# Moving the second-expert matmuls of FFN block 3 behind the third level's second half in a fused RWKV-7 and expert-FFN kernel

## What is computed

```
xn  = layernorm(x)
s   = timemix(xn)             # RWKV-7: mixes, LoRA gates, a recurrence over time, group norm
      S_t = S*decay + (S a) b^T + v k^T ;  y_t = S_t r
g   = silu(ffn(xn))
      top 2 of 8 experts by softmax of xn @ gate_w
      for each chosen expert e:  relu(xn@wi + bi + (xn@A_e)@B_e) @ wo + bo, times the sum of the two scores
```

## Time and profile before

| quantity | value |
|---|---|
| median of 3 runs | 990.77 us (990.7 to 991.04) |
| the profiled execution | 991.04 us, with a span of 989.2 us from first to last instruction |
| PE busy | 973.3 us, 98% of the span |
| DVE busy | 837.0 us, 85% |
| ACT busy | 637.8 us, 64% |
| POOL busy | 441.1 us, 45% |
| granted TensorE clock, mean | 1.000 of full speed (2.4 GHz) |

### The profile page before, as it was taken

The page is one execution under the profiler, slowest core; times in us unless marked ns, Lnnn a source line. Parts: engine busy times, 40 slices in busy tenths (PEclk is TensorE's granted clock), DMA queues, the critical chain, the costliest instruction groups (busy, mean ns, idle before and its releaser), DMA issues.

```text
span 989.2 us, 46773 instructions
## 1 busy us (share of the span) xinstructions
PE 973.3 (98%) x20578; PEld 766.3 (77%) x20578; DVE 837.0 (85%) x1685; ACT 637.8 (64%) x1483; POOL 441.1 (45%) x536
## 2 busy tenths in 40 slices
PE   8999999999999999999999999999999999999997
PEld 5777778787787877777777787877878777787775
DVE  7988979789798897979979798897988979789776
ACT  4765765756757566676656667577575666756655
POOL 4452724427154361634627245372443716346150
PEclk9999999999999999999999999999999999999999
DMA  8000000000000000000000000000000000000000
GB/s 261 14 3 3 4 3 24 4 23 4 17 10 4 24 4 23 4 4 23 4 24 3 3 24 3 24 4 3 24 4 25 3 24 3 4 24 4 13 4 23
DMA packets 9416, 17.28 MB, mean 17 GB/s; under 512 B 1920, under 2 KB 4224, under 8 KB 8960
## 3 DMA queue, kind: packets, MB, share of 16 engines
q1 hardware_dynamic: 9216, 14.30, 4.5%
HBM read 10.10 MB, written 4.19 MB: 14 GB/s over the span
## 4 chain that ended last, share of the span: by engine, by line
PE 95%; DVE 2%; issue 1%; ACT 1%; SPq 0%; DMA 0%; ACTq 0%; DVEq 0%
PE bank L259 34%; PE bank L258 20%; PE grams L474 10%; PE bank L352 5%; PE bank L489 3%; PE bank L500 3%; PE grams L543 2%; PE grams L448 2%; PE grams L598 2%; PE grams L563 2%; PE bank L574 2%; PE bank L533 2%; PE bank L367 2%; PE bank L584 1%; PE bank L383 1%; PE bank L307 1%
## 5 line engine op out<-in xcount | busy, mean ns | idle before, releaser
L1272 POOL TENSOR_TENSOR bk<-bk,tot 128x256 f32<-128x256 f32 x192 | 155.4, 817 | 138.1 <-PE grams L474 138.1
L1594 DVE COPY_PREDICATED gm<-c_mask_g,grams 128x1024 f32<-128x1024 int32 x96 | 161.3, 1680 | 5.7 <-PE grams L474 3.9
L1026 ACT ACTIVATE gl<-gm 32x128 f32<-32x128 f32 x320 | 99.1, 310 | 78.3 <-DVE gm L1594 72.1
L917 ACT ACTIVATE relu<-bank,prm 128x256 f32<-128x256 f32 x256 | 105.7, 472 | 36.7 <-PE bank L259 34.2
L1253 POOL TENSOR_TENSOR xd<-mtmp,xnc 128x512 f32<-128x512 f32 x95 | 121.1, 1276 | 13.1 <-DVE mtmp L1455 11.3
L474 PEld LDWEIGHTS grams<-ar,bk 64*64 64x64 f32 x6144 | 102.2, 134 | 19.5 <-issue 14.4
L259 PE MATMUL bank<-w_wo,hid 128*128 128x256 f32 x488 | 116.1, 386 | 0.0
L474 PE MATMUL grams<-ar,bk 64*64 64x64 f32 x6144 | 110.2, 220 | 0.0
L1604 DVE TENSOR_TENSOR ar<-ar,tot 128x512 f32<-128x512 f32 x96 | 92.5, 964 | 13.2 <-PE grams L474 13.2
L259 PEld LDWEIGHTS bank<-w_wo,hid 128*128 128x128 f32 x488 | 90.1, 190 | 13.1
L259 PE MATMUL bank<-xnc,w_wi 128*128 128x256 f32 x392 | 94.4, 384 | 0.9 <-ACT relu L917 0.9
(11 more groups left out here) (247 smaller groups left out, 2150.8 us busy)
## 6 DMA issues: line engine op xcount, KB each, us to landing
x_in<-x SPq DMA_DIRECT2D x16, 256.0 KB, 2.9
out<-out_t SPq DMA_DIRECT2D x15, 256.0 KB, 2.0
w_wi<-w_wi_dram SPq DMA_DIRECT2D x1, 1024.0 KB, 7.0
w_wo<-w_wo_dram SPq DMA_DIRECT2D x1, 1024.0 KB, 9.3
w_lora_B<-w_lora_B_dram SPq DMA_DIRECT2D x1, 512.0 KB, 8.2
w_x_B<-w_x_B_dram SPq DMA_DIRECT2D x1, 384.0 KB, 3.2
w_kW<-w_kW_dram SPq DMA_DIRECT2D x1, 256.0 KB, 4.4
w_rW<-w_rW_dram SPq DMA_DIRECT2D x1, 256.0 KB, 4.0
```

The source lines that it names most:

```text
L917: A(dst[:, p % 2, j * 256:(j + 1) * 256], ZB[p % 2][:, j * 256:(j + 1) * 256], ACT.Relu, bias=prm[:, P_BI + 2 * p + j:P_BI + 2 * p + j + 1 ...
L1026: A(gl[l % 2][o:o + 32, :, :, :].rearrange("p q g (c n m) -> p (q g c) n m", c=2, m=m), right(gm[o:o + 32, :, :, :, b, 0, 32 * k:32 * k + ...
L1272: tt(v, v, d, ALU.mult).then_inc(S(f"bk{k}_scaled"), 1)
L1594: run(v.copy_predicated(dst, msk.to_broadcast([128, 32, HALF // m, m]), src), "g_stored")
```

## The change

In the branch of steps 2 to 16, PE's `diff(3)` is taken from its place between `gram(4)` and `kW` and put behind `inv_off(3)`, ahead of `gram(5)`. No other engine's order is changed, and no wait is added or removed.

```diff
                     if rec:
                         gram(4)
-                        diff(3)
                     if front:
                         pe.wait_ge(*till("mx_4_done", 2))
                         kW()
                     if rec:
                         inv_x(3)
                     if front:
                         pe.wait_ge(*till("mx_5_done", 2))
                         wk_B()
                     if rec:
                         inv_off(3)
+                        diff(3)
                         gram(5)
                         inv_x(4)
                     if front:
                         pe.wait_ge(*till("kraw_done", 1))
                         pe.wait_ge(*till("ksq_done", 1))
                         g_A()
```

## The result

The changed kernel takes 1032.76 us (median of 4 runs, 1028.41 to 1033.59). The kernel before took 990.9 beside it. The ratio is 1.0407, with a 95% interval of 1.0391 to 1.0424: 4% slower. The forecast was 1020.8, with a range up to 1027. The direction was right and the size too small by 12 us.

What follows compares the result with a forecast made beforehand. PE, never idle in a full step of 60.08 us, was taken as the bound. 14 x 1.97 + 2.38 = 29.96 us on the median of 990.77 gave 1020.8 us, with a range of 1010 to 1027.

Steps and rivals of the forecast that it cites:

- What bounds the kernel: PE is busy for all 60.08 us of a full step, so any wait opened on it is added whole.
- The entry of `diff(3)`: Between `inv_off(3)` and `gram(5)`, `diff(3)` pays its own entry from small tiles: 1.06 us in all, 0.20 added per step.
- a free entry: At `diff(3)`, weight loads pulled ahead could make the entry cost nothing, the sum about 3 us smaller over 15 steps.
- The wait before `inv_off(3)`: PE reaches `inv_off(3)` before DVE's `keep_x(3)` is done and waits about 0.14 us, bounded by 0 and 0.25.
- The queue behind `relu(2, 3)`: On ACT, `pack_gram(4)` and `kraw_` wait behind `relu(2, 3)`, so PE waits 1.04 us before `inv_x(4)` and 0.59 before `g_A`.
- The two waits: PE waits 1.04 us for `gl` before `inv_x(4)` and 0.59 us for `ksq` before `g_A`, 15 times each.
- The total at full clock: 14 steps longer by 1.97 us and step 2 by 2.38, added to the median of 990.77: 1020.8 us.
- "The granted clock stays 1.00": Sign expected in the profile after: PE's granted clock stays at 1.00, with a full step of about 62.05 us.
- The rival in which the clock falls: PE's clock drops to 1.2 GHz around `inv_x(4)` and `g_A`: 22 us over 15 steps, 1042 or more; chance 0.03.
- The range: For the whole kernel's time, 1010 to 1027 us, about 0.87 together; the likeliest case's own range was 1013 to 1026.

Runs made afterwards that it cites:

- the kernel without the queue waits: The changed kernel with ACT's `relu(2, 3)` moved behind `sig_`: 991.32 us, ratio to before 1.0008.
- the four kernels with a filled pause: The changed kernel with useless 256-column matmuls in both of PE's pauses (1018.7 us), the first alone (1020.16), the second alone (1020.42), or half the first (1019.47).

## Why the prediction was right and where it was wrong

- **What bounds the kernel**: right. PE has no idle time in a full step, and every wait that was opened stayed in the total.
- **The entry of `diff(3)`**: right, 1.07 as against 1.06, and `kW` alone 1.92 against 1.93. Against it I had set a free entry, after the Trainium skill's rule on pulled-ahead weight loads ("TensorE: Matmul & The Clock Gate", Part 2: What happens when you issue a matmul). The 0.20 is there, so that reading of the rule doesn't hold for this entry. The rule asks for free rows of the array or the background buffer, and no run here shows whether either was given.
- **The wait before `inv_off(3)`**: its cause right, its size too large. `inv_off(3)` starts 3.35 us after `kW` does (442.95 - 439.60) where 3.48 was worked out. What is left of the 0.14 is 0.02 ahead of it and 0.07 within it, as its piece of the chain lasts 0.45 instead of 0.38. Together with the entry a step grows by 0.28 in the kernel without the queue waits, against 0.34.
- **The queue behind `relu(2, 3)`**: right, and shown by moving one line on ACT. 2.01 us were forecast from the end of `diff(3)`'s matmuls to `gl`, 2.04 measured (444.47 to 446.51). The two waits are 1.10 and 0.58 to 0.61, against 1.04 and 0.59. A step at full clock is 62.2, against 62.05. In step 2 `norm` starts at 68.39, where 68.40 was worked out.
- **The total at full clock**: right, about 1019 to 1020 (both pauses filled, or one), against 1020.8. The extra 0.15 x 15 = 2 us and 3 us fewer of the pauses without a cause nearly cancel.
- **"The granted clock stays 1.00"**: wrong, and this is the miss. The rival in which the clock falls got a chance of 0.03. It is what happened, in 8 of 15 steps, and it costs 12 to 14 us: 1032.76 less 1018.7 to 1020.4 in the four kernels with a filled pause. So the sum lacked a term for the clock. The evidence I held against it was a trace at 1.00 throughout and one row after the end of PE's work, which showed that the clock doesn't fall at once. It said nothing of a stretch in which PE does small pieces between pauses. The kernel before has no such stretch in its full steps, so its trace could not have excluded it, and the chance of the rival was not mine to put at 0.03. Its price was off too, in both directions: I let only `inv_x(4)` and `g_A` run slow, but in every step. In truth `inv_x(4)` is still at full clock, and in the fall shown above all from `g_A` to `norm` is slow, 1.54 us a time, but only in some steps. The Trainium skill's section on frequent short pauses ("TensorE: Matmul & The Clock Gate", A second HAM failure mode: psum-queue depth-cycling) describes this, and here the trace agrees: mean clock 0.985 with pauses of 1.1 and 0.6 us.
- **The range** ended at 1027, since the rival with the clock was left outside. It should have reached to 1042, the price that the text itself gave.

Why some steps keep their clock and others with the same pauses don't is not settled: the order of instructions is the same in them. Nor is the cause of the pauses that carry no releaser, which come to about 4.7 us over 14 steps of the kernel before and to between 0.4 and 1.5 in several of the others.

## What to carry to other kernels

When an instruction is moved later on one engine, look at its reader's own list: what stands behind the reader waits too, needed or not. Count the slack of everything behind it, not of the reader; here the DVE addition that reads `relu(2, 3)` comes more than 10 us later, and `gl`, behind it in the list, had 2.57 us. Where the move leaves TensorE idle for one or two microseconds in a stretch that was dense, price the clock as well, as a case with a real chance, because the trace of a dense kernel can't rule it out; here pauses of 1.1 and 1.37 us per step were free and 1.7 us cost the clock in half of the steps. A quick test for it is useless matmuls in the pause: here they made the changed kernel 14 us faster. They are no cure; taking the neighbours out from behind the waiting reader gave 41 us.

## What the runs showed of the hardware

- In the profiled executions the clock fell from 2.4 to 1.2 GHz in some of steps 2 to 16 of every kernel whose pauses before `g_A` came to 1.7 us or more, in one piece or two (8, 7 and 12 steps), and in none of those steps where they came to 1.37 or less. In step 17 of one kernel it fell after 1.3 us of idle time. A fall cost about 1.5 us (3.93 against 2.39 for the same matmuls).
- A full-array group of matmuls behind 32 x 32 or 64 x 64 tiles took 0.20 us more than behind full-array work (2.79 against 2.59 for twelve instructions, 1.06 against 0.86 for four); 64-column forms took 0.15 there (1.01 for eight), and full-array transposes behind them 0.15 again (0.59 against 0.44).
- A one-column ACT instruction in a row of such cost 0.09 us (three made the pause 0.27 us longer, fourteen 1.3), not the 0.2 to 0.3 that I had allowed for each.
